# Linear attention on one core: the root of the norm on another engine, alternating heads, one state array, and decays by halves

## The chip, the cores and the metric

The kernel runs on one core of a Trainium2 chip. The metric is the device time of one execution in microseconds. PE is the matrix engine (TensorE), DVE the vector engine, ACT the scalar engine, POOL is GpSimd and SP the engine that issues most DMAs. Each engine works through its own instructions in order; semaphores tie them together. All tensors here are 32-bit floats; PE takes such a matmul in two passes, so one matmul of the code is two records of the profile.

## What is computed

Two transformer layers over 4096 tokens of width 256. The change lies in the last block, a gated linear attention with 8 heads of 64 features: a dense state and one state for each of 4 experts, all with the same values `v`. From the reference:

```python
def step(S, inp):                       # over chunks of 64 tokens
    kv, dec, qg_c = inp
    o_inter = jnp.einsum('thd,hde->the', qg_c, S)
    return (S * dec[..., None] + kv, o_inter)
...
o_dense = gla_b(q1, k1, v, gk1)
o_sparse = gla_be(q_e, k_e, v, gk_e).sum(axis=1)   # 4 experts, each token in one
o = o_dense + o_sparse
g = (x @ Wga @ Wgb).reshape(B, L, H, DV)
o = o * lax.rsqrt(jnp.mean(o * o, axis=-1, keepdims=True) + EPS) * norm_w
o = o * (g * jax.nn.sigmoid(g))
return o.reshape(B, L, H * DV) @ Wo
```

## The kernel before

`linear_attention` is the last stage. It goes through 32 tiles of 128 tokens (two chunks of 64, which are the two halves of a tile). It is a software pipeline: every engine has its own function `iteration(nxt, cur, prv)`, and `run` calls it for each tile. In one iteration the engines project and gate tile `nxt`, compute scores, states and output sums of tile `cur`, and normalise, gate and project the output of tile `prv`. The order in each `iteration` is the order in that engine's queue, and it is written by hand.

PE's order (L2424 to L2440): projections Z1, Z2 (pre-gates) of `nxt`; `turn_feats` (transposes of keys and queries of `cur`, with ACT's copies out of the two PSUM buffers `psW` between them); ZG (output gate) and K2; `decay_sums`; `scores` in four parts of four matmuls, x = 0 and 1 dense, x = 2 and 3 for the experts, each part on one half of the array's rows; Q2 and V; `turn_o` of `prv`; `keys_values`; `project_o`; G1, G2 (running sums of the log gates); `intra`; K1, Q1; `inter`. `psP` has two banks, so a projection waits until DVE or ACT has read the one two places before it.

The steps that the change touches:

- The norm. After `inter`, ACT squares the output sums (L2102), DVE sums the squares (L2146) and scales them and adds epsilon (L2148). ACT then makes the root as exp(-0.5 ln) (L2107, L2109), behind `copy_feats` and `log_sigmoids`; Ln and Exp need different tables, so a table load comes before each. DVE multiplies the output sums by it (L2161) and by the gate (L2164), which holds the norm weight (L2262). `turn_o` waits for L2164.
- DVE's order (L2266): `mean_square`, `add_bias` (reads Z1 and Z2; PE's ZG and K2 wait for it), `center` (reads K2), four masks of `mask_scores` (L2182), `gated` (L2161, L2164), `log_sigmoid`, `decay_states`, `add_to_states`, `output`, `scaled`. The second pair of score parts on PE waits for the first pair's masks, since they share `psW`.
- The states. `s1_end`, `s1_mid` (dense) and `s2_end`, `s2_mid` (experts) are separate arrays, each read and written by its own DVE operation in L2209 to L2229. The dense sums `kv1` and the expert sums `psS2` lie in different PSUM tensors.
- `keys_values` (L2394 to L2398): for each head four expert matmuls and a dense one, all into the 64 PSUM partitions of that head's parity, that is on one half of the array's columns.
- `decay_sums` (L2381 to L2385): stationary operand of 128 columns (a pair of heads), moving operand of 2 or 8 columns. ACT takes their exp in `decays` (L2087), after the root.
- `intra` (L2408): per head one matmul of 128 x 128 masked scores with 64 columns of values. ACT's `eg` and `egn` (L2096, L2097) read G1 and G2, and K1 and Q1 wait for them.
- POOL's order (L2035): `queries` (four products of 512 columns, L2008), `half_masks` (L2015), `add_scores` (L2021), `keys` of `nxt` (four products, L2027, from DVE's L2255 on). A `hold` is a semaphore wait and an increment.

## Time and profile before

| | |
|---|---|
| Median of three runs | 5782.2 us (5778.06 to 5784.22) |
| The profiled execution, its own time | 5784.91 us |
| Its span, first to last instruction | 5783.2 us |
| Busy in the span | PE 4961.7 us (86%), DVE 4323.1 (75%), ACT 3136.3 (54%), POOL 938.3 (16%) |
| The steady part of the last stage, 4760 to 5740 us | PE busy 945.91 of 980 us, DVE 770.66, ACT 450.13, POOL 368.01 |

Matmuls are pipelined and their ends are modelled, so a busy PE is not PE at its peak. The granted clock is the share of 2.4 GHz that TensorE got in a stretch: 1.00 is 2.4 GHz, 0.50 is 1.2 GHz, and a mean between them is a mixture of both. "Idle before" in a row is the time for which the engine had nothing running, and after the arrow stands what ended it.

### The profile page before, as it was taken

How to read it: one execution, taken by the hardware profiler on the slowest of the kernel's cores; microseconds unless marked ns; L12 is line 12 of the kernel's file. 1: busy time of each engine (PE TensorE's matmuls, PEld its weight loads, DVE VectorE, ACT ScalarE, POOL GpSimd, SP SyncE). 2: the span in 40 equal slices, each digit the busy share in tenths (PEclk: the TensorE clock that was granted, in tenths of full speed). 3: DMA queues.
4: the chain of work that ended last, by engine and by line, in shares of the span. 5: the costliest groups of instructions: out<-in, count | busy, mean ns of one | idle time of the engine just before them, and what ended most of it. 6: DMA issues, size and time to landing. Idle time of an engine off the chain costs nothing. (4 is left out here: it accounts for less than half of the span.)

```text
span 5783.2 us, 106990 instructions
## 1 busy us (share of the span) xinstructions
PE 4961.7 (86%) x37182; PEld 2607.9 (45%) x37184; DVE 4323.1 (75%) x5246; ACT 3136.3 (54%) x5403; POOL 938.3 (16%) x886
## 2 busy tenths in 40 slices
PE   6589999999999999999932758467999879999998
PEld 3233333333333333333322336235666647677676
DVE  4589999999999999999466223466665557777777
ACT  1068888888888888888921212112222234444443
POOL 0000000000000000000007720443220013334333
PEclk8689999999999999999965879778999969999998
DMA  5322333323322222222111047421110120100000
GB/s 180 109 93 91 100 100 97 98 88 98 103 91 81 77 82 81 82 80 78 32 43 66 14 128 235 147 76 58 54 37 1 59 73 22 26 23 22 26 23 14
DMA packets 241629, 431.82 MB, mean 75 GB/s; under 512 B 37945, under 2 KB 142410, under 8 KB 239008
## 3 DMA queue, kind: packets, MB, share of 16 engines
q1 hardware_dynamic: 197424, 355.18, 19.9%
q0 software_dynamic: 26928, 62.99, 3.4%
q10 hardware_dynamic: 16896, 8.39, 0.6%
q8 instruction: 260, 4.26, 0.3%
q14 instruction: 121, 0.99, 0.1%
HBM read 329.36 MB, written 133.89 MB: 80 GB/s over the span
## 5 line engine op out<-in xcount | busy, mean ns | idle before, releaser
L579 DVE TENSOR_REDUCE attn_mpart<-attn_ps_max 128x2 f32<-128x1024 f32 x2048 | 2498.6, 1225 | 122.6 <-PE attn_ps_max L617 111.1
L524 ACT ACTIVATE attn_probs<-attn_ps_exp 128x512 f32<-128x512 f32 x4096 | 2222.0, 595 | 350.8 <-PE attn_ps_exp L633 103.5
L617 PE MATMUL attn_ps_max<-attn_keys,attn_quer 54*128 54x512 f32 x4096 | 1503.5, 462 | 82.2 <-DMA attn_keys<-k_laid 55.1
L633 PE MATMUL attn_ps_exp<-attn_quer,attn_keys 54*128 54x512 f32 x4096 | 1505.9, 450 | 23.6 <-issue 13.5
L648 PE MATMUL attn_ps_out<-attn_probs,attn_vals 128*32 128x256 f32 x16384 | 1317.7, 393 | 8.4 <-ACT attn_o_sb L530 7.8
L633 PEld LDWEIGHTS attn_ps_exp<-attn_quer,attn_keys 54*128 54x128 f32 x4096 | 615.1, 186 | 877.1 <-ACT attn_probs L524 839.6
L648 PEld LDWEIGHTS attn_ps_out<-attn_probs,attn_vals 128*32 128x32 f32 x16384 | 324.0, 108 | 755.8 <-issue 400.5
L617 PEld LDWEIGHTS attn_ps_max<-attn_keys,attn_quer 54*128 54x128 f32 x4096 | 602.6, 190 | 123.4 <-DVE attn_mpart L579 63.5
L1442 PE MATMUL ra_psO<-ra_vals,ra_probT 128*128 128x256 f32 x1152 | 299.7, 410 | 80.2 <-DVE ra_probT L1614 80.0
L1371 POOL DMA_INDIRECT ra_rows<-y_rows,slots x256 | 253.8, 991 | 379.6 <-DVE ra_total L1536 308.2
L1500 ACT ACTIVATE ra_row<-ra_psS 128x512 f32<-128x512 f32 x112 | 66.9, 597 | 448.7 <-PE ra_psS L1423 448.7
L1442 PEld LDWEIGHTS ra_psO<-ra_vals,ra_probT 128*128 128x128 f32 x1152 | 227.3, 206 | 120.7 <-DVE ra_probT L1614 89.0
L734 POOL DMA_INDIRECT x_rows<-pay,slots x256 | 255.2, 997 | 126.6 <-issue 126.6
L1423 PE MATMUL ra_psS<-ra_kT,ra_qT 128*128 128x512 f32 x576 | 255.7, 598 | 8.8 <-DVE ra_kT L1586 8.8
L2027 POOL TENSOR_TENSOR gla_ke<-gla_kg,emask 128x512 f32<-128x512 f32 x128 | 166.5, 1328 | 535.0 <-DVE gla_kg L2255 535.0
L511 POOL DMA_DIRECT2D x_rows<-attn_zeros x16 | 8.8, 550 | 1412.6 <-ACT attn_o_sb L530 1412.6
L2321 PE MATMUL gla_psP<-gla_wqkv,gla_hc 128*128 128x512 f32 x384 | 220.4, 718 | 11.2 <-ACT gla_egn L2097 11.2
L915 POOL MEMSET route_below<- 128x64 f32 x2 | 0.3, 151 | 1363.9 <-POOLq L55 1363.9
L1614 DVE COPY ra_probT<-ra_psT 128x512 f32<-128x512 f32 x144 | 96.9, 689 | 127.9 <-PE ra_psT L1433 127.4
L1423 PEld LDWEIGHTS ra_psS<-ra_kT,ra_qT 128*128 128x128 f32 x576 | 110.5, 193 | 138.6 <-issue 124.4
L2008 POOL TENSOR_TENSOR gla_qeT<-gla_ftT,gla_emr 128x512 f32<-128x512 f32 x128 | 158.4, 1271 | 70.1 <-ACT gla_ftT L2051 70.1
L2102 ACT ACTIVATE gla_sq<-gla_psO 128x512 f32<-128x512 f32 x32 | 19.1, 597 | 268.1 <-PE gla_psO L2420 268.1
(324 smaller groups left out, 6001.5 us busy)
## 6 DMA issues: line engine op xcount, KB each, us to landing
attn_keys<-k_laid SPq DMA_DIRECT2D x256, 304.0 KB
attn_vals<-v_aug SPq DMA_DIRECT2D x128, 512.0 KB, 15.0
attn_keys<-k_laid SPq DMA_DIRECT2D x256, 128.0 KB
x_rows<-attn_zeros POOLq DMA_DIRECT2D x16, 1280.0 KB, 9.9
exp_x<-x_rows SPq DMA_DIRECT2D x64, 320.0 KB
exp_w1w<-in_w SPq DMA_DIRECT2D x64, 256.0 KB
y_rows<-exp_y SPq DMA_DIRECT2D x64, 256.0 KB
q_laid<-proj_parts SPq DMA_DIRECT2D x32, 256.0 KB
```

Of the source, the lines that this page charges most:

```text
L524: act.activation(probs[k % 2][:, j, :], ps_exp[bank_of(g, n)][:, :], ACT.Exp).then_inc(exp_done, 1)
L579: dve.tensor_reduce(mpart[i][:, kb, TC * pair + tile::TC * NPR], ps_max[u % 2][:, :, :], AX, ALU.max).then_inc(unit_read, 1)
L617: mm = pe.matmul(ps_max[u % 2][:, h, :], quer[g][half(h), pair, tile * P:(tile + 1) * P], keys[g % 2][half(h), pair, kb * CH:(kb + 1) * CH ...
L633: pe.matmul(ps_exp[bank_of(g, n)][:, :], keys[g % 2][half(h), pair, k * P:(k + 1) * P], quer[g][half(h), pair, :], start=True, stop=True). ...
L648: mm = pe.matmul(ps_out[j * VW:(j + 1) * VW, n], vals[:, k, j * VW:(j + 1) * VW], probs[k % 2][:, j, n], start=(k == 0 and q == 0), stop=( ...
L734: pool.indirect_dma_start(out=x_rows, out_offset=bass.IndirectOffsetOnAxis(ap=slots[:, n, k:k + 1].bitcast(U32), axis=0), in_=pay[:, n, :] ...
L1371: pool.indirect_dma_start(out=rows[n % 2][:, k, :], out_offset=None, in_=y_rows, in_offset=bass.IndirectOffsetOnAxis(ap=slots[:, n, k:k + ...
L1423: mm = pe.matmul(psS[g % 2][:, :], qT[s // TC % 2][:, k, s % TC * P:(s % TC + 1) * P], kT[:, k, b * BLK:(b + 1) * BLK], start=(k == 0), st ...
L1442: mm = pe.matmul(psO[s % 2][:, :], probT[(before(s) + b) % 2][:, j * P:(j + 1) * P], vals[:, n, :], start=(n == 0), stop=(n == TC * blocks ...
L2008: last = pool.tensor_tensor(qeT[:, b, :, :], ftT[:, 3, b, :].unsqueeze(1).to_broadcast([P, NE, P]), emr[i][:, :, :], ALU.mult)
L2027: last = pool.tensor_tensor(ke[i][:, e, :], kg2[:, :], emask[:, bass.ds(m, 1), e].to_broadcast([P, KDV]), ALU.mult)
L2321: mm = pe.matmul(ps, hc[i][:, k, :], wqkv[:, x, k, :], start=(k == 0), stop=(k == KD - 1))
```

## The change

The root moves to POOL: ACT's square is scaled by 1/8, so that DVE's sum is the mean already; POOL adds epsilon and raises to the power -0.5, with arrays `eps` and `power` as second operands, at the head of its iteration. DVE's `gated` is split: `scale_o` comes before `add_bias`, the product with the gate right after it. ACT's `decays` stands between Exp and Ln of the log-sigmoid. Dense and expert states become one array `s_end` and `s_mid` with NS = 5 states per head, and their PSUM sums one array of three banks. `scores` and `keys_values` alternate between even and odd heads from matmul to matmul, `decay_sums` and `intra` work in halves of 64 stationary columns that alternate too. The first scores come before the decay sums and the second ones after them; the second pair now waits for both masks of the first. The norm weight is multiplied into the rows of `wo` once, before the loop, and is loaded as one column by two DMAs in place of one.

```diff
-        nw = sb("nw", [P, DK])
+        nw = sb("nw", [P, 1])
...
-        dec1 = dec[:, 0:NPAIR * 2].rearrange("p (a c) -> p a c", c=2)
-        dec2 = dec[:, NPAIR * 2:].rearrange("p (a e c) -> p a e c", e=NE, c=2)
+        s_end, s_mid = sb("s_end", [P, NPAIR, NS, DK]), sb("s_mid", [P, NPAIR, NS, 2, DK])
+        dec = sb("dec", [P, NPAIR, NS, 2])
         sq, on = sb("sq", [P, HL, DK]), sb("on", [P, HL, DK])
-        ms = sb("ms", [P, HL])
+        ms, power, eps = (sb(n, [P, HL]) for n in ("ms", "power", "eps"))
         oT = sb("oT", [P, NPAIR, P])
         ob = two("ob", [P, D])
         psP = pb("psP", [P, 2, KDV])
...
-        pdec2 = pdec[:, NPAIR * 2:].rearrange("p (a e c) -> p a e c", e=NE, c=2)
+        psS = pb("psS", [P, 3 * CH])
+        NKV = NPAIR * NS * DK
+        kv = psS[:, 0:NKV].rearrange("p (a e d) -> p a e d", a=NPAIR, e=NS)
+        pdec = psS[:, NKV:NKV + NPAIR * NS * 2].rearrange("p (a e c) -> p a e c", a=NPAIR, e=NS)
         psO = pb("psO", [P, HL, DK])
         w_loaded = sem("w_loaded")
         loaded = [sem(f"loaded{i}") for i in range(2)]
@@ -1921,14 +1916,14 @@
         (sp_passed, pool_passed, const_set, halves_step, projected, biased, gate_copied, lz_step, ls_ready, k_centered,
          k_exped, k_step, q2_scaled, v_copied, g_exped, sig_ready, dense_ready, sparse_ready, gate_ready, cme_ready,
...
-                                 (nw[:, :], norm_w.partition_broadcast(P))):
+                                 *((nw[rows, :], norm_w.rearrange("(d o) -> d o", o=1))
+                                   for rows in (slice(0, DK), slice(DK, P)))):
...
+                pool.memset(power[:, :], -0.5).then_inc(halves_step, 1)
+                pool.memset(eps[:, :], EPS1).then_inc(halves_step, 1)
...
+                def root(tile):
+                    m, _, i = tile
+                    hold(pool, ms_ready, m + 1, pool_passed)
+                    pool.tensor_tensor(ms[:, :], ms[:, :], eps[:, :], ALU.add).then_inc(eps_added, 1)
+                    hold(pool, eps_added, m + 1, pool_passed)
+                    pool.tensor_tensor(ms[:, :], ms[:, :], power[:, :], ALU.pow).then_inc(rms_ready, 1)
+
                 def iteration(nxt, cur, prv):
+                    if prv is not None:
+                        root(prv)
                     queries(cur)
...
                     act.activation(lz[:, :, :], lz[:, :, :], ACT.Exp, scale=-1.0).then_inc(lz_step, 1)
+                    if cur is not None:
+                        decays(cur)
                     act.wait_ge(lz_step, 3 * m + 2)
                     act.activation(lz[:, :, :], lz[:, :, :], ACT.Ln, bias=1.0).then_inc(lz_step, 1)
...
-                    act.activation(sq[:, :, :], psO[:, :, :], ACT.Square).then_inc(squared, 1)
-
-                def rms(tile):
-                    m, _, i = tile
-                    act.wait_ge(ms_ready, m + 1)
-                    act.activation(ms[:, :], ms[:, :], ACT.Ln).then_inc(rms_step, 1)
-                    act.wait_ge(rms_step, m + 1)
-                    act.activation(ms[:, :], ms[:, :], ACT.Exp, scale=-0.5).then_inc(rms_ready, 1)
+                    act.activation(sq[:, :, :], psO[:, :, :], ACT.Square, scale=DK ** -0.5).then_inc(squared, 1)
...
                     if nxt is not None:
-                        log_sigmoids(nxt)
-                    if prv is not None:
-                        rms(prv)
-                    decays(cur)
+                        log_sigmoids(nxt, cur)
+                    else:
+                        decays(cur)
                     if nxt is not None:
                         q2_and_v(nxt)
                     if prv is not None:
...
+                dve.wait_ge(w_loaded, 112)
+                dve.tensor_scalar(wo[:, :, :], wo[:, :, :], nw[:, 0:1], None, ALU.mult).then_inc(wo_set, 1)
...
-                    dve.tensor_reduce(ms[:, :], sq[:, :, :], AX, ALU.add).then_inc(o_step, 1)
-                    dve.wait_ge(o_step, m + 1)
-                    dve.tensor_scalar(ms[:, :], ms[:, :], 1.0 / DK, EPS1, ALU.mult, ALU.add).then_inc(ms_ready, 1)
+                    dve.tensor_reduce(ms[:, :], sq[:, :, :], AX, ALU.add).then_inc(ms_ready, 1)
...
-                def gated(tile):
+                def scale_o(tile):
                     m, _, i = tile
                     dve.wait_ge(rms_ready, m + 1)
 
                     dve.wait_ge(o_turned, m)
                     dve.tensor_tensor(on[:, :, :], psO[:, :, :], ms[:, :].unsqueeze(2).to_broadcast([P, HL, DK]),
                                       ALU.mult).then_inc(o_read, 1)
+
+                def gated(tile):
+                    m, _, i = tile
...
-                        dve.tensor_tensor(s1_mid[part, :, x, :], s1_end[part],
-                                          dec1[part, :, 0].unsqueeze(2).to_broadcast([DK, NPAIR, DK]), ALU.mult)
-                        last = dve.tensor_tensor(s2_mid[part, :, :, x, :], s2_end[part],
-                                                 dec2[part, :, :, 0].unsqueeze(3).to_broadcast([DK, NPAIR, NE, DK]),
+                        last = dve.tensor_tensor(s_mid[part, :, :, x, :], s_end[part],
+                                                 dec[part, :, :, 0].unsqueeze(3).to_broadcast([DK, NPAIR, NS, DK]),
                                                  ALU.mult)
...
-                        dve.tensor_tensor(s1_end[part], kv1[part], s1_mid[part, :, x, :], ALU.add)
-                        last = dve.tensor_tensor(s2_end[part], psS2[part], s2_mid[part, :, :, x, :], ALU.add)
+                        last = dve.tensor_tensor(s_end[part], kv[part], s_mid[part, :, :, x, :], ALU.add)
...
-                    dve.tensor_tensor(gs[i][:, :], zb[:, 2, :], ls[i][:, 2, :], ALU.mult).then_inc(y_step, 1)
-                    dve.wait_ge(y_step, m + 1)
-                    dve.tensor_tensor(gs[i][:, :].rearrange("p (h d) -> p h d", h=HL),
-                                      gs[i][:, :].rearrange("p (h d) -> p h d", h=HL),
-                                      nw[:, :].unsqueeze(1).to_broadcast([P, HL, DK]), ALU.mult).then_inc(gate_ready, 1)
+                    dve.tensor_tensor(gs[i][:, :], zb[:, 2, :], ls[i][:, 2, :], ALU.mult).then_inc(gate_ready, 1)
...
                 def iteration(nxt, cur, prv):
                     if prv is not None:
                         mean_square(prv)
+                        scale_o(prv)
                     if nxt is not None:
                         add_bias(nxt)
+                    if prv is not None:
+                        gated(prv)
                     if nxt is not None:
                         center(nxt)
                     mask_scores(cur)
-                    if prv is not None:
-                        gated(prv)
                     if nxt is not None:
                         log_sigmoid(nxt)
...
-                pe.wait_ge(w_loaded, 96)
+                pe.wait_ge(w_loaded, 112)
+                pe.wait_ge(wo_set, 1)
...
-                def scores(tile):
-                    m, _, i = tile
-                    pe.wait_ge(feats_copied, 4 * m + 4)
-                    for x in range(4):
-                        if x >= 2:
-                            pe.wait_ge(scores_masked, 4 * m + x - 1)
-
-                        r = x % 2 * DK
-                        for b in range(NPAIR):
-                            mm = pe.matmul(psW[(x + 1) % 2][:, b * P:(b + 1) * P], ftT[r:r + DK, x // 2 * 2, b, :],
-                                           ftT[r:r + DK, x // 2 * 2 + 1, b, :], start=True, stop=True)
-                        mm.then_inc(scores_summed, 1)
+                def scores(tile, kind):
+
+                    m, _, i = tile
+                    if kind:
+                        pe.wait_ge(scores_masked, 4 * m + 2)
+                    else:
+                        pe.wait_ge(feats_copied, 4 * m + 4)
+                    for b in range(NPAIR):
+                        for odd in range(2):
+                            r = odd * DK
+                            mm = pe.matmul(psW[1 - odd][:, b * P:(b + 1) * P], ftT[r:r + DK, 2 * kind, b, :],
+                                           ftT[r:r + DK, 2 * kind + 1, b, :], start=True, stop=True)
+                            if b == NPAIR - 1:
+                                mm.then_inc(scores_summed, 1)
 
                 def project_o(tile, cur):
                     m, _, i = tile
@@ -2379,10 +2377,14 @@
                     pe.wait_ge(kv_read, m)
                     pe.wait_ge(cme_ready, m + 1)
                     for b in range(NPAIR):
-                        pe.matmul(pdec1[:, b, :], ls[i][:, 0, b * P:(b + 1) * P], halves[:, :], start=True, stop=True)
+                        for odd in range(2):
+                            rows, head = slice(odd * DK, odd * DK + DK), slice((2 * b + odd) * DK, (2 * b + odd + 1) * DK)
+                            pe.matmul(pdec[rows, b, 0, :], ls[i][:, 0, head], halves[:, :], start=True, stop=True)
                     for b in range(NPAIR):
-                        mm = pe.matmul(pdec2[:, b, :, :], ls[i][:, 1, b * P:(b + 1) * P], cme[i][:, :, :],
-                                       start=True, stop=True)
+                        for odd in range(2):
+                            rows, head = slice(odd * DK, odd * DK + DK), slice((2 * b + odd) * DK, (2 * b + odd + 1) * DK)
+                            mm = pe.matmul(pdec[rows, b, 1:NS, :], ls[i][:, 1, head], cme[i][:, :, :],
+                                           start=True, stop=True)
                     mm.then_inc(dec_summed, 1)
 
                 def keys_values(tile):
@@ -2391,11 +2393,12 @@
                     pe.wait_ge(ke_ready, m + 1)
 
                     pe.wait_ge(dec_exped, m + 1)
-                    for hh in range(HL):
-                        head, rows = slice(hh * DK, (hh + 1) * DK), slice(hh % 2 * DK, hh % 2 * DK + DK)
-                        for e in range(NE):
-                            pe.matmul(psS2[rows, hh // 2, e, :], ke[i][:, e, head], v[i][:, head], start=True, stop=True)
-                        mm = pe.matmul(kv1[rows, hh // 2, :], kg1[i][:, head], v[i][:, head], start=True, stop=True)
+                    for b in range(NPAIR):
+                        for e in range(NS):
+                            for odd in range(2):
+                                head, rows = slice((2 * b + odd) * DK, (2 * b + odd + 1) * DK), slice(odd * DK, odd * DK + DK)
+                                keys = ke[i][:, e - 1, head] if e else kg1[i][:, head]
+                                mm = pe.matmul(kv[rows, b, e, :], keys, v[i][:, head], start=True, stop=True)
                     mm.then_inc(kv_summed, 1)
 
                 def intra(tile):
@@ -2405,8 +2408,10 @@
 
                     pe.wait_ge(o_read, m)
                     for hh in range(HL):
-                        pe.matmul(psO[:, hh, :], a1[:, hh, :], v[i][:, hh * DK:(hh + 1) * DK],
-                                  start=(hh == 0), stop=False, skip_group_check=True)
+                        for late in range(2):
+                            rows = slice(late * GC, late * GC + GC)
+                            pe.matmul(psO[rows, hh, :], a1[:, hh, rows], v[i][:, hh * DK:(hh + 1) * DK],
+                                      start=(hh == 0), stop=False, skip_group_check=True)
 
                 def inter(tile):
                     m, _, i = tile
@@ -2414,11 +2419,10 @@
                     pe.wait_ge(qe_ready, m + 1)
                     for b in range(NPAIR):
                         o = psO[:, 2 * b:2 * b + 2, :].rearrange("p h d -> p (h d)")
-                        pe.matmul(o, ftT[:, 1, b, :], s1_mid[:, b, :, :].rearrange("p h d -> p (h d)"), start=False,
-                                  stop=False, skip_group_check=True)
-                        for e in range(NE):
-                            mm = pe.matmul(o, qeT[:, b, e, :], s2_mid[:, b, e, :, :].rearrange("p h d -> p (h d)"),
-                                           start=False, stop=(b == NPAIR - 1 and e == NE - 1), skip_group_check=True)
+                        for e in range(NS):
+                            queries = qeT[:, b, e - 1, :] if e else ftT[:, 1, b, :]
+                            mm = pe.matmul(o, queries, s_mid[:, b, e, :, :].rearrange("p h d -> p (h d)"),
+                                           start=False, stop=(b == NPAIR - 1 and e == NE), skip_group_check=True)
                     mm.then_inc(intra_inter, 1)
 
                 def iteration(nxt, cur, prv):
@@ -2426,8 +2430,9 @@
                     ahead(Z1, Z2)
                     turn_feats(cur)
                     ahead(ZG, K2)
+                    scores(cur, 0)
                     decay_sums(cur)
-                    scores(cur)
+                    scores(cur, 1)
                     ahead(Q2, V)
                     if prv is not None:
                         turn_o(prv, cur)
```

## Rows read from the trace of the kernel before

**Rows 1.** windows over the steady part of the last stage; columns: stretch, length, busy us (instructions) of each engine, clock, DMA
```profile
4760.00:5740.00 980.00, 945.91 (x7002) 690.54 (x6999) 770.66 (x1033) 450.13 (x611) 368.01 (x291) 0.92 0.09 23
```

**Rows 2.** the chain that ended last, from 4600 us on, by line
```profile
by line: PE gla_psP L2321 17.0%; PE gla_psO L2420 9.7%; PE gla_psS L2397 9.2%; PE gla_psW L2363 8.8%; PE gla_psP L2325 8.6%; PE gla_psW L2373 5.3%; PE gla_psP L2317 4.9%; PE gla_psW L2341 4.5%; ACT gla_eg L2096 2.8%; issue 2.6%; ACT gla_egn
```

**Rows 3.** windows over four iterations in a row; columns as in rows 1
```profile
5209.62:5241.93 32.31, 29.85 (x240) 22.13 (x239) 25.34 (x36) 15.42 (x21) 12.66 (x11) 1.00 0.11 24
5241.93:5275.39 33.46, 32.80 (x239) 23.94 (x238) 26.57 (x36) 15.50 (x21) 12.66 (x11) 0.90 0.09 24
5275.39:5309.02 33.63, 32.85 (x240) 23.86 (x239) 26.51 (x36) 15.42 (x21) 12.66 (x11) 0.90 0.08 23
5309.02:5342.73 33.71, 32.86 (x240) 23.69 (x239) 26.15 (x36) 15.47 (x21) 12.67 (x11) 0.90 0.11 23
```

**Rows 4.** one window of the second of these iterations; columns as in rows 1
```profile
5248.46:5254.44 5.98, 5.94 (x36) 4.41 (x35) 2.77 (x4) 5.90 (x6) 3.32 (x5) 0.62 0.00 0
```

**Rows 5.** timeline of PE, first iteration; columns: start, length, engine, line, idle before
```profile
5209.62 1.13 PE L2325 MATMUL gla_psP<-gla_wup,gla_lc 16*128 16x512 f32 x4
...
5213.09 1.24 PE L2325 MATMUL gla_psP<-gla_wup,gla_lc 64*128 64x512 f32 x4
5214.26 1.05 PE L2382 MATMUL gla_psS<-gla_halves,gla_ls 128*128 128x2 f32 x8
...
5216.15 1.71 PE L2363 MATMUL gla_psW<-gla_ftT 64*128 64x128 f32 x16
5218.09 1.42 PE L2363 MATMUL gla_psW<-gla_ftT 64*128 64x128 f32 x13 [0.23 <-DVE gla_a L2182]
...
5220.29 1.99 PE L2321 MATMUL gla_psP<-gla_wqkv,gla_hc 128*128 128x512 f32 x4
5223.96 0.65 PE L2350 MATMUL gla_psW<-ident,gla_on 128*128 128x128 f32 x4 [1.68 <-DVE gla_on L2164]
...
5228.09 1.99 PE L2373 MATMUL gla_psW<-gla_wo,gla_oT 128*128 128x256 f32 x8
...
5233.83 3.70 PE L2321 MATMUL gla_psP<-gla_wqkv,gla_hc 128*128 128x512 f32 x8 [0.30 <-ACT gla_egn L2097]
```

**Rows 6.** timeline of DVE, same iteration
```profile
5210.35 0.69 DVE L2146 TENSOR_REDUCE gla_ms<-gla_sq 128x8 f32<-128x512 f32 x1 [0.31 <-ACT gla_sq L2102]
...
5211.88 1.28 DVE L2154 TENSOR_TENSOR gla_zb<-gla_psP,gla_bias 128x512 f32<-128x512 f32 x2
...
5219.28 1.29 DVE L2182 TENSOR_TENSOR gla_a<-gla_psW,gla_m2c 128x512 f32<-128x512 f32 x2 [0.65 <-PE gla_psW L2363]
5222.41 0.69 DVE L2161 TENSOR_TENSOR gla_on<-gla_psO,gla_ms 128x512 f32<-128x512 f32 x1 [1.84 <-ACT gla_ms L2109]
5223.14 0.69 DVE L2164 TENSOR_TENSOR gla_on<-gla_on,gla_gs 128x512 f32<-128x512 f32 x1
```

**Rows 7.** timeline of ACT, same iteration
```profile
5220.87 1.28 ACT L2109 ACT_TABLE_LOAD   x1
```

**Rows 8.** timeline of PE inside keys_values
```profile
5225.05 0.22 PE L2398 MATMUL gla_psS<-gla_v,gla_kg 128*64 128x64 f32 x1
...
5225.11 0.22 PE L2398 MATMUL gla_psS<-gla_v,gla_kg 128*64 128x64 f32 x1
```

**Rows 9.** timeline of POOL, same iteration
```profile
5208.01 3.93 POOL L2027 TENSOR_TENSOR gla_ke<-gla_kg,emask 128x512 f32<-128x512 f32 x3
...
5219.08 0.20 POOL L2015 TENSOR_TENSOR gla_cme<-emask,gla_halves 128x8 f32<-128x8 f32 x1
5220.75 2.34 POOL L2021 TENSOR_TENSOR gla_a<-gla_a 128x1024 f32<-128x1024 f32 x1 [1.46 <-DVE gla_a L2182]
```

**Rows 10.** groups of instructions by line, last stage; columns: count, busy us, mean ns
```profile
L2164 DVE TENSOR_TENSOR gla_on<-gla_on,gla_gs 128x512 f32<-128x512 f32 x32 | 46.5, 1453 | 1.1
```

**Rows 11.** timeline of the last microseconds
```profile
5754.86 1.11 PE L2350 MATMUL gla_psW<-ident,gla_on 128*128 128x128 f32 x4 [3.85 <-DVE gla_on L2164]
...
5772.48 0.69 DVE L2161 TENSOR_TENSOR gla_on<-gla_psO,gla_ms 128x512 f32<-128x512 f32 x1 [2.15 <-ACT gla_ms L2109]
```

More of the change, by code:

```diff
@@ L2041, in iteration @@
                         keys(nxt)
-                run(pool, prologue, iteration, lambda tile: None)
+                run(pool, prologue, iteration, root)
             @block.scalar
@@ L2086, in decays @@
                     act.wait_ge(state_done, m + 1)
-                    act.activation(dec[:, :], pdec, ACT.Exp, scale=GSCALE).then_inc(dec_exped, 1)
+                    act.activation(dec[:, :, :, :], pdec, ACT.Exp, scale=GSCALE).then_inc(dec_exped, 1)
                 def exps(tile):
@@ L2292, in epilogue @@
                     mean_square(tile)
+                    scale_o(tile)
                     gated(tile)
```

36 lines of the change are left out of this document (12 added, 24 removed).

## The prediction, on record before the changed kernel ran

> **What bounds the kernel now.** I read the views from the outside in. The edits touch only the last stage, 32 tiles of 128 tokens from about 4671 us to the end. Of it, the 980 us from 4760 to 5740 are steady repetition, in which PE is busy 945.9 us, DVE 770.7, ACT 450.1 and POOL 368.0 [rows 1]. The chain that ended last runs through PE lines nearly everywhere [rows 2]. So PE's own order of work sets the end, and a saving counts if it shortens PE's work or a wait of PE, and nothing else binds in its place.
>
> Four iterations in a row take 32.31, 33.46, 33.63 and 33.71 us, 133.11 together, 33.28 on average; the 980 us hold 29.4 of them [rows 3]. The first has a mean granted clock of 1.00, the others 0.90. The two levels are 2.4 and 1.2 GHz, so 0.90 means a fifth of the iteration at the lower one, 6.8 us, and 3.4 us of full-speed PE work lost. In the second iteration it lies around the scores: from t = 6.53 to 12.51 the clock is 0.62 [rows 4]. Yet these iterations are only 1.15 to 1.4 us longer. The rest vanishes in waits that PE has anyway, and those waits are what this change touches.
>
> I lay out the undisturbed iteration with t = 0 at its first projection, 5209.62 [rows 5]: ZG and K2 at 3.47, decay sums at 4.64, first half of the scores at 6.53, second half at 8.47, V at 10.67, turn_o at 14.34 after 1.68 us of waiting for DVE's `on`, keys_values about 0.6 later, project_o at 18.47, K1 at 24.21 after 0.30 us of waiting for ACT's egn, and the end at 32.31.
>
> **Why turn_o waits.** DVE's L2161 starts only at 5222.41, released by ACT's `ms`, and the table load for that Exp ends at 5222.15 [rows 6, 7]: the root is queued behind ACT's long log-sigmoid work. `gated` and turn_o come after it. The change takes the root off ACT and puts scale_o and gated early, so this wait goes whole, if nothing else is late by then.
>
> **Alternating heads and split columns.** Z1 and Z2 sit on different row bands, and their four 512-column records take 1.13 us; the eight of K1 and Q1, on the full array, take 3.70, 1.85 for four [rows 5]. Neighbours on different bands overlap. In keys_values two records of one head, so on one column half, start 0.06 us apart [rows 8]; but the 80 records take 3.5 us, 0.044 each, so the seams between heads overlap already. Fully alternated, two streams of 40 at 0.06 give 2.4. Bounds: 3.5 (no gain) and 2.4. I take 2.45, 1.1 us less, since the overlap is already there at each seam.
> The Trainium skill, "TensorE: Matmul & The Clock Gate", Part 1, gives a floor near 25 ns between starts, which would leave room (by it 80 records need 2.0 us), but about 62 ns for each MATMUL where the sequencer decodes in software, by which no order could beat 5 us. The 44 ns of this trace contradict the second.
> Scores: 16 records take 1.71 us from start to end [rows 5]; as two streams of eight at 0.118 (the decay sums' 16 records in 1.89) it is 0.95 until the next stage can start. Decay sums: 32 records of 64 columns in two streams are 16 x 0.06 = 0.96, against 1.89. A change more between row bands and column halves is bounded by the distance of two neighbours, 0.1 us, and left out.
> Intra: 16 records become 32 shorter ones. It gains nothing: K1 waits for egn, which ACT makes from G1 and G2, and intra only lies in that wait. K1 stays 5.74 us behind project_o [rows 5]; what intra saves, some 0.8 us, turns into idle time there.
>
> **The new wait at the top.** scale_o stands ahead of add_bias on DVE and waits for POOL's root. Queued behind it are add_bias, for which PE's ZG and K2 wait, then gated, center and the masks, for which the second scores wait. POOL's ke ends at 5211.94, t = 2.32 [rows 9]; DVE's sum of squares is ready earlier, 5211.04 [rows 6]. The add runs 2.32 to 2.52 (0.20 us is the row of the 128x8 product [rows 9]); the hold after it costs 0.18 (masks end 5220.57, POOL starts 5220.75 [rows 6, 9]). No row shows a power on POOL: the bounds are 0.20 us (same shape) and 2.34 (the largest POOL row here). I take 0.3, as its eight elements are nearest to the 0.20 row. pow ends at 3.0, scale_o runs 3.05 to 3.74, add_bias 3.70 to 4.98; now it ends at 3.54. So ZG slips from 3.47 to 4.43, K2 to 5.03, the first scores come at 6.1, the decay sums at 7.1 to 8.05, where they fill part of PE's wait for the masks.
> On DVE gated follows at 5.0. In these microseconds POOL works on `queries`, and this product takes more in such company: 0.69 us in this iteration with POOL idle, 1453 ns on the mean [rows 6, 10], so about 1.75 where they meet. It ends at 6.75. center's two operations are of scale_o's size, together 1.42, to 8.17; two masks 1.29, to 9.5. The second scores need both and start at 9.55, 1.1 later than now, after PE has stood idle for 1.5. V follows them by 2.20 now, of which 0.3 go with their overlap: 11.45. V's four records take 1.9 (half of K1 and Q1): turn_o at 13.35 with no wait, keys_values 13.95 to 16.4, K1 5.74 later at 22.15, and from K1 to the end 8.10 as now: 30.25. Undisturbed iteration: 30.25 against 32.31, 2.06 less.
>
> **What costs nothing.** ACT keeps two table loads; the second moves behind oT, where ACT waits for G2; with that cover gone it would cost the 1.28 of its row [rows 7]. DVE's dropped operations (L2148, the norm product L2262) and the joined state operations shorten DVE where PE waits for nothing: it is busy 770.7 of 980 us, its one late point is the root. Should inter come to wait for decay_states, each 0.1 us there would count whole. The norm weight in wo is one product before the loop, and one DMA issue more on SP, once, is below what I can resolve.
>
> **The clock.** The thin stretch of PE's work, decay sums and first scores, gets denser scores and shorter sums, but more idle time, so I see no reason for the falls to vanish. But the waits that swallowed 2.0 to 2.2 of the lost 3.4 us are gone (turn_o) or stand before the fall. A disturbed iteration now costs nearly all of it: 33.65. Three in four iterations are disturbed. What the new phase makes of that no row tells; bounds none and all. I take two in three, near the present share.
> Mean: 30.25 + 2/3 x 3.4 = 32.52, 0.76 less; x 29.4 = 22 us.
> The tail: the last full iteration's turn_o waits 3.85 us, which falls to near nothing; the final scale waits 2.15, of which 1.5 go [rows 11]; with keys_values I say 6.
> Sum: 22 + 6 = 28 under the profiled execution's 5784.9: **5757 us**. The median of the runs, 5782.2, is 0.05% below that execution, which changes nothing.
>
> **The rivals.**
> *Few falls of the clock* (0.15). If the denser work keeps the higher level in three of four iterations, the mean is 31.1: 2.18 x 29.4 = 64, with the tail 70: 5715. For it: scores and decay sums shrink from 3.3 to 1.9 us. Against: the idle time grows.
> *A fall in every iteration* (0.15). 33.65, 0.37 more than now, +11, and -6 at the tail: 5790, no difference. For it: 1.5 us idle behind the sums, 1 us ahead of ZG.
> *The root on POOL is slow* (0.15, the other side). pow at 2 us instead of 0.3 puts 1.7 on the chain POOL, scale_o, add_bias, center, masks, second scores, with nothing to hide it: mean 34.2, +28 and -5: 5808, slower. The gain is used up at a pow of 1.2 us, and it is 0.2% slower from 1.6. For it: a power is no plain product. Against: only eight elements a partition.
> *Alternation gives nothing* (0.10). keys_values at 3.5 and the scores as now: +1.6, mean 34.1: 5804. Against: the overlap in rows 5 and 8.
> The forecast has 0.45; a share of disturbed iterations of a half or five in six moves it by 17 us, so its own range is 5735 to 5780. With the rivals, 5700 to 5808. About 0.2%, 12 us, can be told from no change. Faster: 0.41 of the forecast's 0.45, 0.15, and 0.02 of the two next; same 0.19; slower 0.23.
>
> **What would show it.** In the changed profile: turn_o's wait for DVE gone; ZG starting 1 us later against Z1; PE idle before the second scores, released by the masks; keys_values in about 2.5 us; K1 waiting about 1 us for egn; undisturbed iterations near 30.3 us at clock 1.00, the others near 33.6 at 0.90. The prediction is wrong if POOL's pow takes more than 1 us, if K1's wait is absent, if keys_values stays above 3 us, or if the share of disturbed iterations is far from two in three.

## The result: 0.3% slower, where 0.5% faster was forecast

| | before | after |
|---|---|---|
| Median | 5778.06 us (5770.2 to 5784.22, 9 runs) | 5792.9 us (5791.02 to 5797.54, 9 runs) |
| Profiled execution, its span | 5784.91, 5783.2 us | 5791.02, 5789.3 us |
| Mean iteration, the last 28 | 33.32 us | 34.23 us |
| of it at the lower clock | 5.24 us | 9.26 us |

Ratio of the times 1.0029, 95% interval 1.0019 to 1.0039. The forecast was 5757 us and faster, with its own range of 5735 to 5780; 5792.9 lies above that and inside the range with the rivals, 5700 to 5808. The profiled span grew by 6.1 us: the last stage starts 8.2 us earlier (first Z1, the first projection of an iteration, at 4672.8 instead of 4681.0; why, I did not trace), its 31 steps from Z1 to Z1 take 16.4 us more (the last 28 of them 28 x 0.91 = 25.5 more, the first three 9 less), and what follows the last Z1 takes 72.8 instead of 74.8.

Windows of the kernel after, with the columns of rows 1: the steady part, then five iterations in a row, then a stretch inside the second of these.

```profile
4760.00:5740.00 980.00, 874.82 (x7735) 620.93 (x7734) 704.61 (x798) 444.25 (x548) 442.93 (x345) 0.86 0.08 23
5103.78:5134.14 30.36, 26.55 (x271) 18.93 (x270) 23.68 (x28) 15.22 (x19) 13.08 (x12) 1.00 0.09 26
5134.14:5170.40 36.26, 31.96 (x271) 23.06 (x270) 25.52 (x29) 15.45 (x19) 17.19 (x14) 0.81 0.07 22
5170.40:5206.34 35.94, 32.90 (x272) 22.93 (x271) 24.77 (x28) 15.56 (x19) 15.82 (x13) 0.81 0.07 22
5206.34:5236.62 30.28, 26.61 (x271) 18.91 (x271) 23.75 (x28) 15.22 (x19) 13.22 (x12) 1.00 0.09 26
5236.62:5274.43 37.81, 33.47 (x271) 23.94 (x270) 25.42 (x29) 15.55 (x19) 17.07 (x14) 0.77 0.07 21
5139.20:5152.90 13.70, 12.11 (x73) 8.88 (x74) 9.43 (x12) 7.22 (x7) 8.16 (x7) 0.50 0.04 12
```

PE is busy 71 us less in the same 980 us than before [rows 1], and yet the stage is slower. Two kinds of iteration follow each other. The undisturbed one, in which the clock never falls, takes 30.3 us at clock 1.00, 2.0 less than before [rows 3] and what was forecast (30.25). The disturbed one takes 35.8 to 37.8 (three early ones 34.3), against 33.5 to 33.7 before. The last row shows why: for 13.7 us in one piece the clock is 0.50, which is 1.2 GHz all along; before, 6.8 us of a disturbed iteration were at that level.

The timeline of PE after: the undisturbed iteration, then the disturbed one behind it.

```profile
5103.78 1.13 PE L2321 MATMUL gla_psP<-gla_wup,gla_lc 16*128 16x512 f32 x4
...
5109.11 1.29 PE L2321 MATMUL gla_psP<-gla_wup,gla_lc 64*128 64x512 f32 x3 [1.76 <-DVE gla_zb L2153]
...
5113.53 1.16 PE L2360 MATMUL gla_psW<-gla_ftT 64*128 64x128 f32 x16 [0.78 <-DVE gla_a L2184]
...
5117.30 0.60 PE L2346 MATMUL gla_psW<-ident,gla_on 128*128 128x128 f32 x4
5117.83 0.34 PE L2401 MATMUL gla_psS<-gla_v,gla_kg 128*64 128x64 f32 x4
...
5120.31 1.99 PE L2371 MATMUL gla_psW<-gla_wo,gla_oT 128*128 128x256 f32 x8
...
5126.05 3.70 PE L2317 MATMUL gla_psP<-gla_wqkv,gla_hc 128*128 128x512 f32 x8 [0.95 <-ACT gla_egn L2106]
...
5134.14 1.13 PE L2321 MATMUL gla_psP<-gla_wup,gla_lc 16*128 16x512 f32 x4
...
5140.79 2.67 PE L2321 MATMUL gla_psP<-gla_wup,gla_lc 64*128 64x512 f32 x4 [3.10 <-DVE gla_zb L2153]
5142.66 2.51 PE L2360 MATMUL gla_psW<-gla_ftT 64*128 64x128 f32 x16
```

The first row of each iteration is Z1, the first L2321 row on 64*128 is ZG. turn_o (L2346) has no wait any more, where it had 1.68 us [rows 5]. keys_values (L2401) takes 2.48 us until project_o starts. K1 waits 0.95 us for egn. And ZG waits: 1.76 us in the undisturbed iteration, 3.10 in the disturbed one. The clock falls at 5139.2, inside that wait, 5.1 us after Z1, and what follows takes longer: ZG and K2 2.67 instead of 1.72, the first scores 2.51 instead of 1.65. Only the falls of an iteration behind an undisturbed one start there, 5.0 to 5.2 us after Z1 (5.8 in one early iteration). In a disturbed iteration behind another disturbed one ZG waits 1.7 to 1.8 us and starts at 5.3, and the fall comes at 6.4 to 6.9, 1.1 to 1.6 us later; it lasts 10.2 or 13.7 us all the same.

What ZG waits for, in the timelines of POOL and then of DVE:

```profile
5103.62 2.03 POOL L2025 TENSOR_TENSOR gla_ke<-gla_kg,emask 128x512 f32<-128x512 f32 x2
5105.61 0.20 POOL L2036 TENSOR_TENSOR gla_ms<-gla_ms,gla_eps 128x8 f32<-128x8 f32 x1
5105.99 1.65 POOL L2038 TENSOR_TENSOR gla_ms<-gla_ms,gla_power 128x8 f32<-128x8 f32 x1 [0.18 <-POOL gla_ms L2036]
...
5132.67 4.76 POOL L2025 TENSOR_TENSOR gla_ke<-gla_kg,emask 128x512 f32<-128x512 f32 x4 [14.12 <-DVE gla_kg L2252]
5137.39 0.20 POOL L2036 TENSOR_TENSOR gla_ms<-gla_ms,gla_eps 128x8 f32<-128x8 f32 x1
5137.77 1.65 POOL L2038 TENSOR_TENSOR gla_ms<-gla_ms,gla_power 128x8 f32<-128x8 f32 x1 [0.18 <-POOL gla_ms L2036]
```

```profile
5107.76 0.69 DVE L2160 TENSOR_TENSOR gla_on<-gla_psO,gla_ms 128x512 f32<-128x512 f32 x1 [2.56 <-POOL gla_ms L2038]
5108.37 1.28 DVE L2153 TENSOR_TENSOR gla_zb<-gla_psP,gla_bias 128x512 f32<-128x512 f32 x2
5109.57 0.72 DVE L2166 TENSOR_TENSOR gla_on<-gla_on,gla_gs 128x512 f32<-128x512 f32 x1
...
5116.89 3.27 DVE L2190 SCALAR_TENSOR_TENSOR gla_ls<-gla_zb,gla_lz 128x1536 f32<-128x1536 f32 x1 [0.88 <-ACT gla_lz L2075]
...
5131.80 0.69 DVE L2252 TENSOR_TENSOR gla_kg<-gla_kx,gla_egn 128x512 f32<-128x512 f32 x1
...
5139.44 0.69 DVE L2160 TENSOR_TENSOR gla_on<-gla_psO,gla_ms 128x512 f32<-128x512 f32 x1 [3.88 <-POOL gla_ms L2038]
```

The power takes 1.65 us (0.3 was taken), and the whole chain ke, add, hold, power, scale_o, add_bias stands ahead of ZG. The root starts 1.83 us after Z1 in the undisturbed iteration and 3.25 in the one behind it. That one is late because its ke is: the undisturbed iteration is short, DVE is the engine that is behind in it (it has no idle time of note from 5116.89 on, and the 3.27 us of L2190 there are 1.5 more than in the long iteration), and so L2252, which feeds ke, starts only 2.34 us ahead of the next Z1. In the long iteration DVE waits 0.92 us for PE near its end, and the same operation starts at 5166.65, 3.75 us ahead of the next Z1. So the fast iteration itself makes the root of the next one late.

Waits of the kernel after in the 980 us: total us, times, longest.

```profile
DVE gla_on L2160 <- POOL gla_ms L2038: 86.3, 29, 3.9
PE gla_psP L2321 <- DVE gla_zb L2153: 63.4, 29, 3.1
PE gla_psP L2317 <- ACT gla_egn L2106: 26.5, 28, 0.9
PE gla_psW L2360 <- DVE gla_a L2184: 7.0, 9, 0.8
```

PE's wait for add_bias is 63.4 us in the 29 iterations, 2.2 each. The chain that ended last now runs through POOL, which it did not touch before [rows 2]:

```profile
by line: issue 13.2%; PE gla_psP L2317 12.8%; POOL gla_ke L2025 7.9%; PE gla_psP L2321 7.6%; PE gla_psW L2360 7.3%; PE gla_psS L2401 4.9%; POOL gla_ms L2038 4.3%; PE gla_psW L2371 3.7%; PE gla_psP L2313 3.4%; DVE gla_s_end L2223 2.5%; DVE g
```

### The profile page after: what moved, and what is told of

It is laid out like the page before. It is cut to its first block and busy times, and to the rows that moved or that the text cites. A ratio compares the mean times of both kernels' runs of the same rounds, so it can differ in the third digit from the quotient of the medians.

```text
span 5789.3 us, 108890 instructions
## 1 busy us (share of the span) xinstructions
PE 4893.8 (85%) x38206; PEld 2540.4 (44%) x38208; DVE 4270.8 (74%) x5021; ACT 3128.5 (54%) x5335; POOL 1023.6 (18%) x952
## 5 line engine op out<-in xcount | busy, mean ns | idle before, releaser
L2025 POOL TENSOR_TENSOR gla_ke<-gla_kg,emask 128x512 f32<-128x512 f32 x128 | 152.2, 1217 | 476.9 <-DVE gla_kg L2252 476.9
L2321 PE MATMUL gla_psP<-gla_wup,gla_lc 64*128 64x512 f32 (+1 forms) x320 | 157.9, 781 | 89.4 <-DVE gla_zb L2153 67.9
L2006 POOL TENSOR_TENSOR gla_qeT<-gla_ftT,gla_emr 128x512 f32<-128x512 f32 x128 | 172.8, 1380 | 14.1 <-ACT gla_ftT L2058 14.1
```

Source lines behind the costliest of these rows:

```text
L2025: last = pool.tensor_tensor(ke[i][:, e, :], kg2[:, :], emask[:, bass.ds(m, 1), e].to_broadcast([P, KDV]), ALU.mult)
L2321: mm = pe.matmul(ps, lc[i][r:r + rows, b, :], wup[r:r + rows, b, :], start=True, stop=True)
```

## The experiments

They ran on three chips: e1 to e4 on one, a_changed and e5 to e7 on the second, e8 to e11 on the third. On each of them the kernel before takes 5943 to 5951 us, not 5778, since what comes before the last stage takes longer (the first Z1 of the changed kernel at 4840 instead of 4673 us). The last stage is the same there: the changed kernel again, **a_changed**, has a mean iteration of 34.07 us. So times are compared as ratios to the kernel before on the same chip, and iterations directly. The first Z1 lies anywhere from 4826 to 4868 us in kernels that differ only in the last stage, which is 0.7% of the time; for small differences the iterations say more than the ratios.

> The changed kernel itself again, beside the three that follow on the same chip. Its ratio to the kernel before was 1.0029; both theories expect 1.001 to 1.005, about 34.2 us per iteration and 9.3 us of it at the lower clock.

Measured: 1.002 (1.0006 to 1.0034).

Mean iteration and lower clock are those of the last 28 iterations of one profiled execution, in us; "undisturbed" is a typical iteration without a fall.

| kernel | ratio to before (95%) | mean iteration | undisturbed | lower clock per iteration |
|---|---|---|---|---|
| changed, again | 1.002 (1.0006 to 1.0034) | 34.07 | 30.3 | 8.8 |
| e1_mult | 0.9866 (0.984 to 0.9891) | 30.74 | 30.23 | 1.8 |
| e2_bias_first | 0.9961 (0.9947 to 0.9975) | 32.96 | 29.56 | 7.6 |
| e3_late_gate | 0.9937 (0.9913 to 0.996) | 32.33 | 31.24 | 3.2 |
| e4_early_only | 1.0326 (1.0301 to 1.0351) | 39.49 | none | 14.8 |
| e5_filler8 | 0.995 (0.9933 to 0.9968) | 33.07 | 30.28 | 5.2 |
| e6_keys_later | 0.9849 (0.9816 to 0.9882) | 31.01 | 30.05 | 2.8 |
| e7_gate_mid | 0.9759 (0.9726 to 0.9792) | 28.62 | 27.97 | 1.2 |
| e8_mid_keys | 0.9777 (0.9743 to 0.9811) | 29.05 | 28.83 | 0.9 |
| e9_kv_by_head | 0.9798 (0.9763 to 0.9833) | 29.39 | 29.04 | 0.7 |
| e10_intra_whole | 0.9746 (0.9711 to 0.9782) | 28.64 | 27.97 | 1.2 |
| e11_mid_mult | 0.9718 (0.9687 to 0.9748) | 28.26 | 27.97 | 0.6 |

### The power itself: e1_mult

```diff
-pool.tensor_tensor(ms[:, :], ms[:, :], power[:, :], ALU.pow)
+pool.tensor_tensor(ms[:, :], ms[:, :], power[:, :], ALU.mult)
```

> The changed kernel with the second POOL operation of the root a multiplication in place of the power (the scale of the output is then wrong, the work is the same but for this operation). The power took 1.65 us in the changed kernel's trace, the addition of the same shape 0.20. Theory A (the late root makes PE idle ahead of ZG, and this idle time lengthens the falls of the clock): the root is ready 1.45 us earlier, PE's wait for add_bias falls from 1.8 to 3.1 us to under 1.7, the falls shorten from 13.7 or 17 us to 7 or 10, and the time comes to 5725 to 5750. Theory B (the alternating, halved matmuls themselves bring the clock down, the wait is a bystander): low-clock time per iteration stays near 9 us, and only the wait's own 1.45 us go in the disturbed iterations: 5765 to 5785.

The timeline of POOL and DVE with the product:

```profile
5231.75 0.20 POOL L2038 TENSOR_TENSOR gla_ms<-gla_ms,gla_power 128x8 f32<-128x8 f32 x1 [0.18 <-POOL gla_ms L2036]
5232.07 0.69 DVE L2160 TENSOR_TENSOR gla_on<-gla_psO,gla_ms 128x512 f32<-128x512 f32 x1 [2.42 <-POOL gla_ms L2038]
```

The ratio, 0.9866, would be 5701 us on the chip of the first comparison (0.9866 x 5778). That is more than theory A had (5725 to 5750), and the falls are shorter than its 7 to 10 us; theory B is out. 1.45 us less on POOL take 3.3 us off the mean iteration and next to nothing off the undisturbed one of the steady pattern. The gain is in the falls of the clock: every second iteration has one still, at 5.0 us after Z1, but of 3.4 us instead of 13.7, and it takes 31.20 us.

PE's wait ahead of ZG did not shrink by 1.45. The iterations are short now, so ke is late in all of them and the root starts at 3.15 to 3.26. The wait is 1.6 us in nearly every iteration, where it was 1.7 and 3.1 by turns, 2.2 on the mean:

```profile
PE gla_psP L2321 <- DVE gla_zb L2153: 39.9, 25, 1.7
```

One undisturbed iteration of e1, early in the stage, has its root at 1.83 as in the kernel after. There PE waits 0.32 and the iteration takes 28.93 us, 1.35 less than the 30.28 with the power:

```profile
4987.66 1.29 PE L2321 MATMUL gla_psP<-gla_wup,gla_lc 64*128 64x512 f32 x3 [0.32 <-DVE gla_zb L2153]
```

### PE kept busy in the wait: e5_filler8

```diff
 turn_feats(cur)
+for x in range(8):
+    pe.matmul(psS[:, NKV + 64:NKV + 64 + P], ident[:, :], ident[:, :], start=True, stop=True)
 ahead(ZG, K2)
```

> The changed kernel with eight 128 x 128 products of the identity, 1.8 us at full clock, put on PE ahead of ZG, into the stretch in which it waits for add_bias; they write columns of the state sums' bank that nothing reads. Theory A (the idle time ahead of ZG brings the clock down early and long): low-clock time per iteration falls from 9.3 us to 6 or less, the falls at t = 5 to 6.5 go, and the kernel is faster with more work, 32 to 33 us per iteration, ratio to the kernel before 0.988 to 0.997. Theory B (the idle time is a bystander): low-clock time stays near 9, and the time does not fall; ratio 1.002 to 1.008.

```profile
5199.90 1.95 PE L2433 MATMUL gla_psS<-ident 128*128 128x128 f32 x16
5203.13 1.29 PE L2321 MATMUL gla_psP<-gla_wup,gla_lc 64*128 64x512 f32 x3 [1.28 <-DVE gla_zb L2153]
```

PE does 1.95 us more that nobody needs. ZG starts no earlier than in the changed kernel: 6.6 us after Z1 in this iteration, 6.4 to 6.6 in four others of the last 28, 5.3 in the rest, where the added products fill the wait whole. And the kernel is 0.7% faster than the changed one on the same chip, as theory A had it. The falls come 10 to 12 us after Z1 and last 3.4 or 6.8 us. Nothing else was altered, and the root starts where it did, so PE's idle time ahead of ZG, and not the lateness of ZG, is what makes the falls early and long. By the Trainium skill, "TensorE: Matmul & The Clock Gate", Part 1, an idle array loses its clock and busy time brings it back; the runs agree (8.8 us at the lower level per iteration with the gap, 5.2 with most of it filled).

### The order on DVE: e2_bias_first, e7_gate_mid

```diff
 # e2: add_bias ahead of scale_o
-mean_square(prv); scale_o(prv); add_bias(nxt); gated(prv); center(nxt)
+mean_square(prv); add_bias(nxt); scale_o(prv); gated(prv); center(nxt)
 # e7: scale_o and gated between the masks
-mean_square(prv); scale_o(prv); add_bias(nxt); gated(prv); center(nxt); mask_scores(cur)
+mean_square(prv); add_bias(nxt); center(nxt); mask_scores(cur, (0, 1)); scale_o(prv); gated(prv); mask_scores(cur, (2, 3))
```

> The changed kernel with DVE's add_bias ahead of scale_o, so that PE's ZG and K2 no longer stand behind the root; all work is kept. Theory A: PE's wait ahead of ZG goes whole (1.8 to 3.1 us), low-clock time per iteration falls from 9.3 us to 5 or less, and the time comes to 5700 to 5735. Theory B: low-clock time stays near 9 us per iteration, 5755 to 5785.

> The changed kernel with scale_o and gated on DVE between the first two masks and the last two, behind add_bias and center: neither PE's ZG nor its second scores then stand behind the root, and turn_o still finds its operand ready. Theory A: PE's waits ahead of ZG and of the second scores shrink to under 1 us, an undisturbed iteration takes 28 to 29 us, the falls are at most 6.8 us, 29 to 31 us per iteration, ratio 0.975 to 0.987. Theory B (alternation and halves bring the clock down by themselves): low-clock time of 7 us or more per iteration stays, 31 to 32.5 us, ratio 0.987 to 0.995.

With add_bias first ZG has no wait for it, and yet e2 missed theory A. Its 0.9961 would be 5755 us on the first chip, at the edge of theory B's range and not A's 5700 to 5735, and 7.6 us per iteration are at the lower level, between the two. Both had left out that the wait moves to the second scores, whose masks are still behind scale_o; the falls now come at 7.8 to 10 us after Z1:

```profile
5142.06 2.08 PE L2360 MATMUL gla_psW<-gla_ftT 64*128 64x128 f32 x16 [2.67 <-DVE gla_a L2184]
```

With the gate behind the first two masks the wait ahead of ZG is gone and the one ahead of the second scores is 0.81, as in the undisturbed iteration of the changed kernel (0.78). A window of one undisturbed iteration of e7, and its PE:

```profile
5272.27:5300.25 27.98, 25.89 (x272) 18.40 (x271) 23.33 (x28) 15.11 (x19) 12.78 (x11) 1.00 0.10 28
```

```profile
5275.77 1.13 PE L2322 MATMUL gla_psP<-gla_wup,gla_lc 64*128 64x512 f32 x4
...
5279.64 1.16 PE L2361 MATMUL gla_psW<-gla_ftT 64*128 64x128 f32 x16 [0.81 <-DVE gla_a L2184]
```

ZG starts 3.50 us after Z1, the second scores 7.37 after it (9.75 in the changed kernel), and turn_o 11.1 after it without a wait, though the gate now comes later on DVE. Four of five iterations have no fall. It is 2.4% faster than the kernel before (0.9726 to 0.9792), and faster than the changed kernel, e2 and e3.

### Parts alone: e3_late_gate, e4_early_only

e3 is the changed kernel with the root on ACT and the old place of the gate; e4 is the kernel before with the early gate (POOL's root, scale_o ahead of add_bias, decays between Exp and Ln) and nothing else.

```diff
 # e3, DVE                                   # e3, ACT
-mean_square; scale_o; add_bias; gated; center; mask_scores
+mean_square; add_bias; center; mask_scores; scale_o; gated
+rms(prv)   # Ln, Exp behind log_sigmoids, then decays
 # e4, DVE of the kernel before
-mean_square; add_bias; center; mask_scores; gated
+mean_square; scale_o; add_bias; gated; center; mask_scores
```

> The changed kernel without its early gate: root on ACT by Ln and Exp behind the log-sigmoid, DVE's order and ACT's order as before the change; alternation, the joined state array, halves and the norm weight in wo stay. Theory A: nothing waits ahead of ZG, the falls are 6.8 us again and are partly absorbed by turn_o's wait, an undisturbed iteration takes about 31.2 us: 5740 to 5760, faster than before the change. Theory B: low-clock time per iteration is 9 us or more as in the changed kernel, and the time is 5780 or above.

> The kernel before with the early gate alone: root on POOL, scale_o ahead of add_bias, gated behind it, decays between Exp and Ln; no alternation, no joined array, no halves. Theory A: the wait ahead of ZG and the long falls appear here too, low-clock time 9 us or more per iteration, and without the shorter matmuls the time is 5810 to 5850. Theory B: low-clock time stays at the 5.2 us of the kernel before, and the time is 5770 to 5800.

The rest of the change alone is worth 1.0 us per iteration (33.32 to 32.33) and 0.6% of the time, as theory A had it, and the time at the lower level falls from 5.2 to 3.2 us: alternation and halves do not bring the clock down. The early gate alone costs 3.3%. That would be 5966 us on the first chip: theory A has the direction, but its 5810 to 5850 is far too small. Its wait, in e4:

```profile
5190.64 1.72 PE L2332 MATMUL gla_psP<-gla_wup,gla_lc 64*128 64x512 f32 x4 [2.22 <-DVE gla_zb L2156]
```

No iteration of e4 is undisturbed; the falls come 5 to 8.4 us after Z1 and last 10.2 to 17.1 us. Why the same gate costs 6.2 us per iteration here and 1.9 on top of e3 (32.33 to 34.23), I did not settle.

### An earlier root: e6_keys_later, e8_mid_keys

```diff
 # POOL
-root(prv); queries(cur); half_masks(nxt); add_scores(cur); keys(nxt)
+root(prv); keys(cur); queries(cur); half_masks(nxt); add_scores(cur)
```

> The changed kernel with POOL's four products ke moved from the end of one iteration to behind the root of the next, so that the root no longer stands behind them; keys_values needs them only at t = 14. Theory A: the root starts at about 1.5 instead of 1.9 to 3.3 and always alike, PE's wait ahead of ZG is 1.3 to 1.5 us instead of 1.8 to 3.1, the long falls get rarer, 31.5 to 33 us per iteration, ratio to the kernel before 0.985 to 0.997. If instead the wait for the power itself (1.65 us) is enough for the long falls, they stay and the ratio is 0.997 to 1.003.

> The gate in the middle of the masks and POOL's keys behind the root, together. Theory A (the root's lateness costs only through DVE's order): with the gate in the middle nobody waits for the root any more, so the earlier root buys nothing: ratio to before 0.976 plus or minus 0.002, undisturbed iterations 27.95 to 28.05 us. Rival B (POOL's order has a worth of its own, through its company with DVE): another 0.3% or more off, 0.973 or less.

In e6 the root starts 1.6 us after Z1 in every iteration, ZG waits 1.5, and the falls of the steady part are 3.4 us long: 1.5% faster than before, a little better than theory A's 0.985 to 0.997 and 31.5 to 33 us. On top of e7 the same move costs: undisturbed iterations take 28.83 instead of 27.97. Neither theory had that, though the ratio, 0.9777, lies within theory A's and cannot be told from e7's. The row shows a new wait, since keys now stand ahead of add_scores, and intra needs its result:

```profile
5297.32 1.15 PE L2412 MATMUL gla_psO<-gla_v,gla_a 128*64 128x64 f32 x32 [1.80 <-POOL gla_a L2019]
```

It takes the place of K1's wait of 0.95; the difference, 0.85, is the 0.86 that the iteration grew.

### Prices of single steps on top of e7: e9_kv_by_head, e10_intra_whole, e11_mid_mult

```diff
 # e9: by head                                       # e10: undivided
-for b in pairs: for e in range(NS): for odd in range(2): kv matmul
+for b in pairs: for odd in range(2): for e in range(NS): kv matmul
-for late in range(2): pe.matmul(psO[rows, hh, :], a1[:, hh, rows], v)
+pe.matmul(psO[:, hh, :], a1[:, hh, :], v)
 # e11: pow -> mult on POOL, as in e1
```

> The gate in the middle, and keys_values by head as before (five products of one head, then the next head). Theory A (the alternation is worth its full price, as nothing between keys_values and K1 hides it): keys_values 3.5 instead of 2.5 us, undisturbed iterations 29.0 instead of 27.97, ratio 0.976 + 1.0 x 31 / 5944 = 0.981. Rival B (order gives nothing, or a wait swallows it): 0.976, iterations 28.0.

> The gate in the middle, and the intra products undivided as before (8 of 128 rows instead of 16 of two halves). Theory A, that of the prediction (intra lies in K1's wait for ACT's egn): intra 0.8 us longer, K1's wait 0.95 shrinks to 0.15, iterations stay at 27.97, ratio 0.976. Rival B (it counts): 28.8 us and 0.980.

> The gate in the middle, and a product in place of the power on POOL (the scale of the output differs; nothing else). Theory A (the power costs only where DVE waits for it): 1.45 us less on POOL, no change: ratio 0.974 to 0.978, undisturbed iterations 27.97. Rival B (the power costs POOL time that comes back later, in queries or add_scores): 0.3% or more faster.

In e9 keys_values takes 3.55 us from its first row to project_o, K1 waits 0.95 as before, and the iteration takes 29.04:

```profile
5299.49 0.33 PE L2402 MATMUL gla_psS<-gla_v,gla_kg 128*64 128x64 f32 x2
...
5303.04 1.99 PE L2372 MATMUL gla_psW<-gla_wo,gla_oT 128*128 128x256 f32 x8
```

So the alternation is worth 1.07 us per iteration, all of it on the path. In e10 K1's wait is 0.30 instead of 0.95 and the iteration is the same:

```profile
5164.61 3.70 PE L2318 MATMUL gla_psP<-gla_wqkv,gla_hc 128*128 128x512 f32 x8 [0.30 <-ACT gla_egn L2106]
```

Intra in halves gains nothing, as predicted. In e11 undisturbed iterations are the same 27.97: off the path the power costs nothing there. The ratio, 0.9718, lies below theory A's 0.974 to 0.978 and below that of e7, with intervals that overlap, and the mean iteration is 0.36 shorter, by fewer falls; that is too little to call, so rival B is not excluded.

## Why the prediction was wrong

Right, with size:
- turn_o's wait is gone (1.68 before, none). keys_values 2.48 (2.45 was taken); e9 confirms that its gain counts whole. K1's wait for egn 0.95 (about 1). Intra gains nothing (e10).
- The undisturbed iteration: 30.3 (30.25). That number is luck. Inside it errors cancelled: the power was 1.35 us longer than taken and ZG starts at 5.33 instead of 4.43; but ke ended 0.5 earlier, and gated took 0.72 instead of 1.75. POOL was at work on `queries` by then (from 5108.47), but gated began at 5109.57, 0.12 us ahead of POOL's second product, and that product took 1.73 us, where its neighbours took 1.26. The second scores start at 9.75 (9.55), K1 at 22.27 (22.15).
- The share of disturbed iterations: 19 of the last 28, 0.68 (two in three).

**The step that failed** is the one on the clock: "A disturbed iteration now costs nearly all of it: 33.65", with its 6.8 us at the lower level carried over from the kernel before. The 19 disturbed iterations take 36.08 us on average ((28 x 34.23 - 9 x 30.32) / 19) with 13.7 at the lower level, 5.8 us over the undisturbed one and not 3.4. That a disturbed iteration pays nearly all of the lost work was right (5.8 of 6.8); that the fall keeps its length was not. That term alone is 0.68 x 2.4 x 28 = 46 us; with it at its forecast size the kernel would have come out faster. I had seen the new wait ahead of ZG and priced it as a delay. It is worse than a delay: it is idle time of PE at a place where it had none, and the falls start in it or 1.1 to 1.6 us behind it and last twice as long. e5 shows that directly, more work on PE and less time; e1 and e6 show it by shortening the wait, e7 by removing it.

**Terms mis-sized.** The power: 1.65 us, not 0.3. The bound of 2.34 had it in reach; I took the row of the same shape, but that was a product. With 1.65 in its place the prediction's own sum gives 1.35 x 29.4 = 40 us more, 5797, close to the 5791 of the profiled execution; but that would be the right time from the wrong iterations, 31.6 and 35.0 us instead of 30.3 and 36.1. And the root's start: not always at 2.3 after Z1, but at 1.8 or at 3.25, since ke of a short iteration ends late. The tail: 2.1 us instead of 6, and the final scale still waits 2.24 us, now for POOL, where it waited 2.15 for ACT [rows 11]:

```profile
5778.36 0.69 DVE L2160 TENSOR_TENSOR gla_on<-gla_psO,gla_ms 128x512 f32<-128x512 f32 x1 [2.24 <-POOL gla_ms L2038]
```

**The rivals.** "The root on POOL is slow" gave a mean iteration of 34.2 and 5808 us, and 34.23 was measured. Its number was met by luck: it has about 31.95 us for the undisturbed iteration and 35.35 for the disturbed one, and 30.3 and 36.1 were measured. Its mechanism, the power on a chain with nothing to hide it, is real (e1's iteration of 28.93 against 30.28), but ke and gated came out 1.5 us better in that iteration and cancelled it. On the mean the slow power costs 3.3 us per iteration (e1), more than twice its length, and the larger part of that comes by way of the clock. "A fall in every iteration" did not occur. "Alternation gives nothing" is refuted by e9.

What stays open: e4's size, and what decides between a fall of 10.2, 13.7 and 17.1 us.

## What to carry to other kernels

Before putting an operation early in an engine's order, look at what stands behind it there: here scale_o gained 1.7 us for turn_o and made ZG, which had no wait, wait for another engine's result; two masks' worth later it served turn_o just as well, and 0.3% slower became 2.4% faster. Where the trace shows the clock falling, idle time on PE isn't priced at its length: a wait that went from 2.2 to 1.6 us on the mean was worth 3.3 us per iteration (e1). And a saving that makes one iteration short can make a helper engine late in the next; look at two iterations in a row, not at one.

## What the hardware showed that I had not expected

- POOL's power on 128 x 8 elements takes 1.65 us (32 of them, 1648 ns on the mean), eight times the 0.20 us of an addition of that shape. Groups by line of the kernel after, count, busy us and mean ns:

```profile
L2038 POOL TENSOR_TENSOR gla_ms<-gla_ms,gla_power 128x8 f32<-128x8 f32 x32 | 52.7, 1648 | 5.8 <-POOL gla_ms L2036 5.7 <-ACT gla_ftT L2058 0.2
L2036 POOL TENSOR_TENSOR gla_ms<-gla_ms,gla_eps 128x8 f32<-128x8 f32 x32 | 6.3, 198 | 10.9 <-DVE gla_ms L2147 10.9
```

- DVE and POOL hold each other up when both read two arrays. In the undisturbed iteration POOL's add_scores (L2019) starts first and takes its 2.35 us, and DVE's log_sigmoid (L2190) beside it takes 3.27. In the disturbed one log_sigmoid starts first and takes 1.75, add_scores takes 3.69, and the first operation of decay_states (L2211) behind it 3.63 instead of 1.48. POOL and DVE, the undisturbed iteration and then the disturbed one:

```profile
5116.19 2.35 POOL L2019 TENSOR_TENSOR gla_a<-gla_a 128x1024 f32<-128x1024 f32 x1 [2.15 <-DVE gla_a L2184]
5120.09 2.98 DVE L2211 TENSOR_TENSOR gla_s_mid<-gla_s_end,gla_dec 64x1280 f32<-64x1280 f32 x2
...
5150.22 1.75 DVE L2190 SCALAR_TENSOR_TENSOR gla_ls<-gla_zb,gla_lz 128x1536 f32<-128x1536 f32 x1
5150.48 3.69 POOL L2019 TENSOR_TENSOR gla_a<-gla_a 128x1024 f32<-128x1024 f32 x1 [5.54 <-DVE gla_a L2184]
5151.89 5.13 DVE L2211 TENSOR_TENSOR gla_s_mid<-gla_s_end,gla_dec 64x1280 f32<-64x1280 f32 x2
```

Each time the later of the two ends 1.62, 2.20 and 1.35 us behind the earlier one, about what it takes alone (1.75, 2.35, 1.48). In the kernel before neither of these DVE operations met add_scores: it ended before log_sigmoid began. The Trainium skill, "SBUF — State Buffer", describes the port that both share as locked for a whole instruction, the loser blocked; these rows agree.

- 80 records on alternating column halves run in 2.48 us, 31 ns each, against 44 in the old order.
